# Adapter-addressed loads issued by GpSimd, a reordered start, and two small tables placed last, in a fused two-layer LoRA kernel

## The reference

```
x1  = x + (x @ B0[id0[n]].T) @ A0[id0[n]].T
out = x1 + x1 @ W.T + b + 2 * (x1 @ A1[id1[n]]) @ B1[id1[n]]
```

## Time and profile before

| | before |
|---|---|
| median of 3 runs | 1461.14 us (1460.78 to 1465.53) |
| the profiled execution, its own time | 1460.86 us |
| its span in the trace | 1459.1 us |
| TensorE busy | 1405.0 us |
| VectorE, ScalarE, GpSimd busy | 940.4, 485.7, 0.2 us |
| mean granted TensorE clock | 0.987 |
| bytes moved | 308.37 MB, 211 GB/s |

### The profile page before, as it was taken

The page is one execution under the profiler, slowest core; times in us unless marked ns, Lnnn a source line. Parts: engine busy times, 40 slices in busy tenths (PEclk is TensorE's granted clock), DMA queues, the critical chain, the costliest instruction groups (busy, mean ns, idle before and its releaser), DMA issues.

```text
span 1459.1 us, 15911 instructions
## 1 busy us (share of the span) xinstructions
PE 1405.0 (96%) x5992; PEld 1132.3 (78%) x5992; DVE 940.4 (64%) x991; ACT 485.7 (33%) x491; POOL 0.2 (0%) x4
## 2 busy tenths in 40 slices
PE   3699699999999999999999999999999999999999
PEld 2477478788888888888888888888888888888887
DVE  4587367878676665666656766566666666656662
ACT  3234244433223343333233334332323333332231
POOL 0000000000000000000000000000000000000000
PEclk9799799999999999999999999999999999999999
DMA  8799666899897444456856444457765444357642
GB/s 300 256 334 341 221 222 225 289 363 344 257 355 264 130 143 142 162 188 203 259 199 203 144 135 154 142 181 234 240 208 196 145 154 141 133 177 241 187 164 80
DMA packets 104112, 308.37 MB, mean 211 GB/s; under 512 B 13284, under 2 KB 17508, under 8 KB 104036
## 3 DMA queue, kind: packets, MB, share of 16 engines
q1 hardware_dynamic: 104036, 307.36, 63.1%
HBM read 251.73 MB, written 55.57 MB: 211 GB/s over the span
## 4 chain that ended last, share of the span: by engine, by line
PE 91%; SPq 4%; DVE 2%; issue 1%; DMA 1%; ACT 0%; ACTq 0%
PE acc L495 27%; PE acc L497 27%; PE acc L496 27%; PE acc L479 2%; PE down_ps L465 2%; PE down_ps L466 2%; SPq L343 1%; DMA bg_raw<-w_rows 1%; PE image_ps L447 1%; PE image_ps L448 1%; PE image_ps L449 1%; DVE bg_lo L657 1%; SPq L374 0%; SPq L372 0%; DVE w_one L626 0%
## 5 line engine op out<-in xcount | busy, mean ns | idle before, releaser
L495 PE MATMUL acc<-x_hi,w_hi 128*128 128x512 f32 x1792 | 713.1, 398 | 31.7 <-DVE x_lo L652 17.2
L497 PE MATMUL acc<-x_hi,w_lo 128*128 128x512 f32 x1792 | 709.6, 396 | 0.0
L496 PE MATMUL acc<-x_lo,w_hi 128*128 128x512 f32 x1792 | 709.1, 396 | 0.0
L529 ACT ACTIVATE w_hi<-w_one 128x1024 fp32r<-128x1024 f32 x224 | 237.5, 1060 | 707.2 <-PE acc L497 658.8
L495 PEld LDWEIGHTS acc<-x_hi,w_hi 128*128 128x128 f32 x1792 | 339.2, 189 | 114.5 <-issue 15.2
L496 PEld LDWEIGHTS acc<-x_lo,w_hi 128*128 128x128 f32 x1792 | 338.9, 189 | 80.5 <-issue 1.2
L497 PEld LDWEIGHTS acc<-x_hi,w_lo 128*128 128x128 f32 x1792 | 338.5, 189 | 80.3
L630 DVE TENSOR_TENSOR w_lo<-w_one,w_hi 128x1024 fp32r<-128x1024 f32 x224 | 273.6, 1222 | 110.6 <-ACT w_hi L529 95.8
L652 DVE TENSOR_TENSOR x_lo<-x_stage,x_hi 128x1024 fp32r<-128x1024 f32 x80 | 96.1, 1221 | 46.1 <-ACT x_hi L547 46.1
L693 DVE SCALAR_TENSOR_TENSOR sums<-acc,bias_sb,sums 128x512 f32<-128x512 f32 x128 | 95.6, 747 | 44.8 <-PE acc L479 44.6
L547 ACT ACTIVATE x_hi<-x_stage 128x1024 fp32r<-128x1024 f32 x80 | 83.4, 1056 | 111.3 <-DVE x_stage L646 82.6
(11 more groups left out here) (44 smaller groups left out, 543.4 us busy)
## 6 DMA issues: line engine op xcount, KB each, us to landing
w_one<-w_sums SPq DMA_DIRECT2D x120, 512.0 KB, 3.3
w_one<-w SPq DMA_DIRECT2D x104, 512.0 KB, 5.2
x_stage<-x SPq DMA_DIRECT2D x64, 512.0 KB, 4.5
out<-sums SPq DMA_DIRECT2D x128, 256.0 KB, 4.4
w_two<-w SPq DMA_DIRECT2D x40, 512.0 KB, 8.0
w_sums<-w_one SPq DMA_DIRECT2D x40, 512.0 KB, 6.5
resident<-x SPq DMA_DIRECT2D x32, 512.0 KB, 6.3
bg_raw<-w_rows SPq DMA_DIRECT2D x32, 512.0 KB, 5.7
```

Of the source, the lines that this page charges most:

```text
L495: pe.matmul(ps[:, :], w_hi[ws][:, c, :], hi, start=(c == 0), stop=False)
L496: pe.matmul(ps[:, :], w_hi[ws][:, c, :], lo, start=False, stop=False)
L497: mm = pe.matmul(ps[:, :], w_lo[ws][:, c, :], hi, start=False, stop=(c == H - 1))
L529: act.activation(w_hi[s % W_PARTS][:, :, :], w_one[s % W_ONES][:, :, :], ACT.Copy).then_inc(w_hi_ready, 1)
```

## The change

Adapter-addressed loads get a queue of their own, on GpSimd; SP keeps all others. The start is put in another order, and the two tables move to the end of SBUF, behind a pad of 1024 bytes of a partition that keeps them off the early tiles.

```diff
-        bias_sb = sb("bias_sb", [P, C], F32)
-        ids_sb = sb("ids_sb", [1, 2, NB], I32)
         sums = [sb(f"sums{k}", [P, H, T], F32) for k in range(2)]
...
         rank_sum = sb("rank_sum", [2 * R, T], F32)
+        sb("after_images", [P, T // 2], F32)
+        bias_sb = sb("bias_sb", [P, C], F32)
+        ids_sb = sb("ids_sb", [1, 2, NB], I32)
...
-        adapters_loaded = sem("adapters_loaded")
+        a0_loaded = sem("a0_loaded")
+        a1_loaded = sem("a1_loaded")
```

SP loses `adapter`, `load_down`, `load_rank`, `load_rows` and their calls. What is left of its start, and all of GpSimd's program (the four functions are the old ones with `pool` for `sp`):

```diff
             load_w(1)
-            sp.wait_ge(ids_loaded, 2 * DMA)
-            for n in range(NB):
-                ... (16 loads of A0 and A1)
-            sp.dma_start(mask_sb[:, :], mask).then_inc(mask_loaded, DMA)
             for z in background(1):
                 load_bg(z)
             load_w(2)
-            load_rows(0)
+            sp.dma_start(mask_sb[:, :], mask).then_inc(mask_loaded, DMA)
             sp.dma_start(bias_sb[:, :], bias).then_inc(bias_loaded, DMA)
             keep_sum(0)
...
+        @block.gpsimd
+        def _(pool):
...
+            pool.dma_start(ids_sb[:, 0, :], ids0).then_inc(ids_loaded, DMA)
+            pool.dma_start(ids_sb[:, 1, :], ids1).then_inc(ids_loaded, DMA)
+            pool.wait_ge(ids_loaded, 2 * DMA)
+            for n in range(NB):
+                pool.dma_start(a0_raw[:, n, :, :], adapter(0, n, a0_down)...).then_inc(a0_loaded, DMA)
+            for n in range(NB):
+                pool.dma_start(a1_raw[:, n, :, :], adapter(1, n, a1)...).then_inc(a1_loaded, DMA)
+            for half in range(2):
+                load_rows(half)
+            for s in range(STEPS):
+                g, i, o = where(s)
                 if s + 4 in FIRST:
                     load_down(FIRST[s + 4])
                 if i + 1 in RANKED and o == 3:
                     load_rank(g, i + 1)
```

TensorE does step 1, with its first two image chunks, ahead of the `across` product:

```diff
             step(0)
-            pe.wait_ge(adapters_loaded, 2 * NB * DMA)
+            step(1)
+            pe.wait_ge(a0_loaded, NB * DMA)
             pe.wait_ge(a1_ready, 1)
             (the 16 matmuls of L513)
-            for s in range(1, STEPS):
+            for s in range(2, STEPS):
```

ScalarE and VectorE, in their new order:

```diff
 ScalarE
             for r in range(CH):
                 split_x(0, r)
-            act.wait_ge(adapters_loaded, 2 * NB * DMA)
-            (copy of A1, high part of A0)
+            split_w(1)
+            act.wait_ge(a0_loaded, NB * DMA)
+            (high part of A0)
+            for z in background(1):
+                split_bg(z)
+            act.wait_ge(a1_loaded, NB * DMA)
+            (copy of A1)
             (the loop does not split W 1 and the chunks of step 1 again)
 VectorE
             split_w(0)
+            sum_x(0, 1)
             split_x(0, 0)
-            for r in range(1, CH):
-                sum_x(0, r)
-                split_x(0, r)
+            sum_x(0, 2)
+            split_x(0, 1)
+            sum_x(0, 3)
+            split_x(0, 2)
+            split_x(0, 3)
             sum_w(1)
+            split_w(1)
             (memset, low part of A0)
-            dve.wait_ge(bias_loaded, DMA)
+            sum_w(2)
+            for z in background(1):
+                split_bg(z)
```

More of the change, by code:

```diff
@@ L419, in _, with adapter, load_down, load_rank @@
                     sp.dma_start(images[:, T * j:T * (j + 1)], image[:, :]).then_inc(image_stored, DMA)
-                    if j == 1:
-                        load_rows(1)
+            for s in (STEPS - 2, STEPS - 1):
+                store(s)
+            for o in range(H):
+                sp.wait_ge(out_stored[o], DMA * 4 * GROUPS)
+        @block.gpsimd
+        def _(pool):
+            def adapter(layer, n, table):
+                a = pool.value_load(ids_sb[0:1, layer, n:n + 1], min_val=0, max_val=table.shape[0] - 1)
+                return table[bass.ds(a, 1)]
+            def load_down(n):
+                if turn(n):
+                    pool.wait_ge(down_ready, turn(n))
+                pool.dma_start(down_raw[0][:, :, :], adapter(0, n, b0).rearrange("u p c r -> (u p) c r"))\
+                    .then_inc(down_loaded, DMA)
+                pool.dma_start(down_raw[1][:, :, :], adapter(1, n, a1).rearrange("u p c r -> (u p) c r"))\
+                    .then_inc(down_loaded, DMA)
+            def load_rank(g, i):
+                side, half = rank_side(i)
+                n, cols = 2 * g + side, slice(D // 2 * half, D // 2 * (half + 1))
+                if rank_number(g, i):
+                    pool.wait_ge(rank_ready, rank_number(g, i))
+                pool.wait_ge(image_stored, DMA * 4)
+                up = adapter(1, n, b1).rearrange("u r d -> (u r) d")[:, cols]
+                for row in range(0, 96, 2 * R):
+                    pool.dma_start(rank_raw[row:row + R, :], images[R * n:R * (n + 1), cols])\
+                        .then_inc(rank_loaded, DMA)
+                    pool.dma_start(rank_raw[row + R:row + 2 * R, :], up).then_inc(rank_loaded, DMA)
+            def load_rows(half):
+                if half:
+                    pool.wait_ge(image_ready, 2)
+                cols = slice(D // 2 * half, D // 2 * (half + 1))
+                for n in range(NB):
+                    rows = slice(R * n, R * (n + 1))
+                    pool.dma_start(a0_rows[rows, :], adapter(0, n, a0).rearrange("u r d -> (u r) d")[:, cols])\
+                        .then_inc(rows_loaded, DMA)
+                    pool.dma_start(b1_rows[rows, :], adapter(1, n, b1).rearrange("u r d -> (u r) d")[:, cols])\
+                        .then_inc(rows_loaded, DMA)
+            pool.dma_start(ids_sb[:, 0, :], ids0).then_inc(ids_loaded, DMA)
+            pool.dma_start(ids_sb[:, 1, :], ids1).then_inc(ids_loaded, DMA)
+            pool.wait_ge(ids_loaded, 2 * DMA)
+            for n in range(NB):
+                pool.dma_start(a0_raw[:, n, :, :], adapter(0, n, a0_down).rearrange("u p c r -> (u p) c r"))\
+                    .then_inc(a0_loaded, DMA)
+            for n in range(NB):
+                pool.dma_start(a1_raw[:, n, :, :], adapter(1, n, a1).rearrange("u p c r -> (u p) c r"))\
+                    .then_inc(a1_loaded, DMA)
+            for half in range(2):
+                load_rows(half)
+            for s in range(STEPS):
+                g, i, o = where(s)
@@ L425, in _ @@
                     load_rank(g, i + 1)
[L426 to L429, removed]
         @block.tensor
@@ L591, in _ @@
                 split_x(0, r)
[L592 removed]
+            split_w(1)
+            act.wait_ge(a0_loaded, NB * DMA)
+            act.activation(a0_hi[:, :, :, :], a0_raw[:, :, :, :].rearrange("p n c r -> p c n r"), ACT.Copy)\
+               .then_inc(a0_hi_ready, 1)
+            for z in background(1):
+                split_bg(z)
+            act.wait_ge(a1_loaded, NB * DMA)
             act.activation(a1_cols.rearrange("p (c n r) -> p c n r", c=C, n=NB),
                            a1_raw[:, :, :, :].rearrange("p n c r -> p c n r"), ACT.Copy).then_inc(a1_ready, 1)
[L595 to L596 removed]
             for s in range(STEPS):
@@ L599, in _ @@
                 p = PRODUCTS * g + i
-                if s + 1 < STEPS:
+                if 1 <= s < STEPS - 1:
                     split_w(s + 1)
@@ L605, in _ @@
                     copy_down(LAST[s - 1])
-                for z in background(s + 1):
-                    split_bg(z)
+                if s:
+                    for z in background(s + 1):
+                        split_bg(z)
                 if s - 1 in LAST:
@@ L691, in complete @@
                 tile, f = sums[(2, 1, 2, 0)[i - 3]][:, o, :], H * rank_side(i)[1] + o
+                if rank_number(g, i) == 0 and o == 0:
+                    dve.wait_ge(bias_loaded, DMA)
                 dve.wait_ge(rank_done, H * rank_number(g, i) + o + 1)
@@ L743, in _ @@
                     add_down(LAST[s - 1])
-                sum_w(s + 2)
-                for z in background(s + 1):
-                    split_bg(z)
+                if s:
+                    sum_w(s + 2)
+                    for z in background(s + 1):
+                        split_bg(z)
                 if s >= 1:
                     complete(s - 1)
-                if s == 1:
+                if s == 2:
                     dve.wait_ge(across_done, 1)
```

## The result

The changed kernel took **1416.51 us** (median of 4 runs, 1414.85 to 1419.0) against 1461.56 before, a ratio of 0.969 with a 95% interval of 0.966 to 0.971: 45 us faster. The forecast was 1434 with a range of 1422 to 1447, so the sign was right, and the gain was larger than its best end. The profiled execution took 1417.38 us, span 1415.7.

The account below looks back on a forecast made before the run. TensorE's gapless matmul pace was taken as the bound, with time to win only at the start and in steps 12 and 13. 1460.9 - 17 (start) - 9.4 (B1 rows) = 1434.5, given as 1434, range 1422 to 1447.

Parts of the forecast that it names:

- The two tables: Tables moved to the end of SBUF: worth nothing, from matmul durations of 394 and 395 ns in front and behind.
- nothing from 176 us to the last matmuls can give much: Steady stage: TensorE runs without a gap at 0.2326 us per matmul, and the change touches no matmul's shape.
- The start: Up to step 2: it starts at 43 in place of 60.0, 17 us saved, 13 to 21.
- GpSimd's pitch: Time between adapter loads on GpSimd: taken as 1.63 us, bounds 1.15 and 2.89.
- the other estimate: GpSimd's adapter loads: pitch of 1.55 us from the skill's first-byte times, 0.4 more in a load than on SP.
- load_rows(1): B1 rows, steps 12 and 13: on GpSimd 28.2 us, 6.2 late; 9.4 of the 17.9 us lost are saved.
- At 1.15 it is 20.5 us, in time: B1 rows at the lower pitch bound: they land before TensorE needs them, and all 17.9 us are saved.
- Queue and order together: Start and third image block, without the tables: 17 us saved at the start and 9.4 at the B1 rows.
- GpSimd far slower: Rival, adapter loads on GpSimd: pitch from 2.3 us on makes the kernel slower, 1490 at 2.89; chance 0.07.
- The DMA engines as the bound: Rival, start and steps 2 to 16: 12.7 saved at the start, steps 0.3 us longer, 1443; chance 0.15.
- The change doing less than it says: Rival: step 2 starts at 55, GpSimd's rows as late as SP's, 5 to 8 us left, 1454; chance 0.05.
- The tables: Rival, matmul pace: moving them changes it by 2 to 5 ns either way, 12 to 30 us; chance 0.03.

Follow-up runs that it names:

- tables_only: Kernel before with only the pad and the two tables moved to the end: 1434.41 us, ratio 0.981.
- all_but_tables: Changed kernel with the two tables put back between down and sums: 1446.69 us, ratio 0.990.
- queue_only: Kernel before with the adapter-addressed loads issued by GpSimd instead of SP, other engines' order and tables left alone: 1453.07 us, ratio 0.993.
- ring2048: Changed kernel with the scratch area of GpSimd's queue doubled from 1024 to 2048 bytes of a partition: 1410.06 us, ratio 0.965.
- gap64: Kernel before with the two tables moved to the end and 64 unused bytes of a partition where they stood: 1446.36 us.
- gap256: Kernel before with the two tables moved to the end and 256 unused bytes of a partition where they stood: 1433.33 us.

## Why the prediction was wrong, point by point

**The step that failed: "The two tables ... So the 128 bytes are worth nothing".** They are worth 28.6 of the 45 us (`tables_only`). The term was put at nothing, and the bound was read the same way: "nothing from 176 us to the last matmuls can give much: the change touches no matmul's shape". It did not touch the shape, and the pace went from 0.2326 to 0.2271. I compared the mean durations of L465 and L495, 394 and 395 ns. The durations overlap, so they are no pace, as the text itself said elsewhere; and the L465 matmuls come four at a time between those of a step. In the changed kernel both lines fell together:

```profile
L502 PE MATMUL acc<-x_hi,w_hi 128*128 128x512 f32 x820 | 319.5, 390 | 0.0
...
L472 PE MATMUL down_ps<-bg_hi,down 128*128 128x512 f32 x64 | 24.9, 389 | 0.0
```

though neither operand of L472 was moved against the other. The starts say the same: from one of the four to the next it is 0.232 us before and 0.227 to 0.228 in `tables_only`. An equal duration of a short group inside a long one therefore said nothing of its own operands. Why the four take on the pace of their neighbours is open; the distance of a matmul's own two tiles does not explain it. I did give the tables a rival, "12 to 30 us" for 2 to 5 ns, but a chance of 0.03. At the granted clock of 0.50 the matmuls of these traces start 0.427 us apart, which is 512 columns at 1.2 GHz; at 2.4 GHz the same would be 213 ns. The pace of 0.2326 in the earlier trace rows is 19 ns above that, and I never asked what those 19 ns were; that was the row to start from.

**The start: 17 saved was forecast, 7.6 came.** Step by step: TensorE starts at 14.23 (14.25 forecast). Step 1 starts at 25.84 (23.3 to 25.6); x landed late, the sums waited 0.39, 0.59 and 1.68 us for it. Chunk 0 at 33.53 (29 to 32) after 6.0 us of waiting (4 to 6); what it waited for was A0, whose last load went out only at 21.67, and not `W` 2, as the text had it. Then the mis-sized term: A1 was to land by 36, and its copy could start only at 44.07. Two pauses of 5.3 and 6.1 us are most of it; besides, the first load went out at 8.8 and not at 5, and a load took 5.9 us to land and not 2. The product of L521 then waited 3.3 us and ran 6.56 at clock 0.54, more than the 5.44 taken as the most. In `all_but_tables` it ran 3.81 behind a wait of 2.7, and step 2 starts at 48.98: some 3 us of the miss hang on whether the clock fell there. With the pauses removed step 2 starts at 44.2, within the 39 to 47 given.

**GpSimd's pitch: 1.63 was taken, 1.14 measured**, the lower bound from SP's own sequence, and under the 1.55 of the other estimate too. The bounds held for a single load, and an even pitch was the wrong model: pauses of 5 to 7 us, which no row of before could show, cost what the pitch did not.

**`load_rows(1)`: a second term was mis-sized, the 2.1 us from issue to landing.** That row came from SP's loads, which went out while SP's other loads stood behind them. On GpSimd they run beside those. The DMA engines in the two stretches, before and after, then the landing of L415 and the wait in the changed kernel:

```profile
141.80:160.50 18.70, 12.00 (x52) 9.35 (x50) 7.89 (x8) 4.13 (x4) 0.00 (x0) 0.90 0.37 106
```

```profile
122.60:149.20 26.60, 20.37 (x90) 16.49 (x88) 17.70 (x17) 9.73 (x10) 7.76 (x16) 0.97 1.02 317
...
DMA to landing us min/median/max: 2.7/5.7/6.8
...
153.54 2.04 PE L462 MATMUL image_ps<-b_rows,across 128*128 128x512 f32 x2 [10.58 <-DMA b_rows<-b]
```

From the image block (written at 120.80 + 0.68) to the last issue it is 27.2 us, one pause included, and 4.9 more until TensorE can go on: 32.1, where 28.2 was forecast. That is 3.9 of the 4.4 by which the wait of 10.6 is longer than the 6.2 forecast; the faster pace is only the other 0.5, and `queue_only`, at the old pace, waits 10.5 too. It also answers "At 1.15 it is 20.5 us, in time": `ring2048` has no pause, its last load takes 6.9 us from issue until TensorE goes on, and 4.2 us of waiting are left. Of the two waits there the second, for the background tile, did go, as forecast.

**Nothing for the rest.** No wait for the bias, none for the rows of the first block, none in the steady stage for the loads that moved: as forecast.

**Queue and order together: 26.4 forecast, 16.4 measured** (`all_but_tables`, 1446.69). In its profiled execution, whose span is 17.7 us shorter than that of before, 11.0 come by step 2 and 6.7 behind it, of 17 and 9.4 forecast. So both parts were too high, and this part alone, at 1446.7, would have stood just inside the upper end of 1422 to 1447. The place of the tables then carried the kernel below the lower end.

**The rivals.** GpSimd far slower: no, 1.14 us a load. The DMA engines as the bound: from 100 to 130 us they ran at a share of 1.01 and 362 GB/s beside a TensorE without a gap, so they were close to it; that they were not it in steps 2 to 16 does not make them free, since the landing times above grew with their load. The change doing less than it says: in part. Step 2 came at 52.4 (55 in the rival) and GpSimd's rows were no earlier for TensorE than SP's (10.6 us of waiting against 7.5), but the wait for the background tile behind them went, and 16.4 were saved and not 5 to 8. The tables: yes, at the upper end of the size given.

## What to carry to other kernels

Where TensorE's pace is above columns over clock in a stage without a gap, look at where its tiles lie: here two 64-byte tables between the weight tiles and the moving tiles cost 2% of the kernel, and 64 bytes alone 0.9% (`gap64` against `gap256`); putting them last cost no time. Read pace from counts over time, never from overlapping durations. When loads move to GpSimd, try a larger scratch area for its queue, take the time from issue to landing from loads at the DMA share that they will meet, and give a change of order its worth only together with the queue that feeds it.

## What the runs showed of the hardware that I had not expected

In this kernel the pace of back-to-back 128x512 float32r matmuls, each with new weights, depends on the distance between the tiles that they stream and the tiles of the weights: 0.227 us at 0 and 256 bytes, 0.2326 at 128, 0.229 at 64 (400 / 1744). It is the same whether x or `W` is moved by 128, and all moved together keep the good pace. That it repeats with 256 bytes was tried only with 64, 128 and 256. What in the chip does this no run here shows, nor what the 14 ns are that stay above 213.

GpSimd's queue issues loads with an address from a register as fast as SP's does (1.14 against 1.15 us), but with a scratch area of 1024 bytes it stood for 5 to 6 us before the eighth and before the sixteenth 128-partition load. With 2048 bytes 16 such loads in a row went out without a pause.

From issue to landing the 16 loads of A0 rows took a median of 2.1 us on SP, with the DMA engines at a share of 0.55 (29 to 46 us) and 0.37 beside them, and 5.7 on GpSimd, at 0.82 (39.4 to 58.5 us) and 1.02. No run separates the path from the load on the engines, but at the start, where SP too met a share of 0.94 (8 to 26 us), its A0 loads took a median of 5.8 and GpSimd's 5.7, so I take it to be the load.
